# Attention layer in fp32 on one core: orders at both ends of the slot loop, and the tail's row work dealt out anew

## The reference

```python
Q = split_heads(query @ Wq + bq)
K = split_heads(key @ Wk + bk)
V = split_heads(value @ Wv + bv)
attn = softmax(einsum('bhqd,bhkd->bhqk', Q, K) / np.sqrt(D_K))
ctx = einsum('bhqk,bhkd->bhqd', attn, V).transpose(0, 2, 1, 3).reshape(B, S, D_MODEL)
out = ctx @ Wo + bo
return _layer_norm(out + query, ln_gamma, ln_beta)
```

## Time and profile before

| | us |
|---|---|
| median of 3 runs | 647.02 (645.25 to 647.41) |
| profiled execution | 653.13, its span 651.3 |
| last matmul ends | 632.3 |
| last GpSimd instruction ends | 648.05 |
| chain that ended last, over the span | GpSimd 37%, TensorE 31%, issue 18% |
| one slot in the middle | about 8.25 |

### The profile page before, as it was taken

One profiled execution on the slowest core, in us unless ns is written; L12 is line 12 of the kernel. 1 busy time (PEld: TensorE's weight loads), 2 busy tenths in 40 slices (PEclk: granted clock), 3 DMA queues, 4 the chain that ended last, 5 costly groups with the idle time before them and its releaser, 6 DMA issues.

```text
span 651.3 us, 12015 instructions
## 1 busy us (share of the span) xinstructions
PE 602.2 (92%) x3336; PEld 438.8 (67%) x3336; DVE 498.8 (77%) x909; ACT 361.7 (56%) x667; POOL 452.8 (70%) x401
## 2 busy tenths in 40 slices
PE   6989878999899999999999999999999999998980
PEld 5978645677676776777777777767777677675660
DVE  5523467888688888888888888888888888687655
ACT  5611145466466666666666666666666666554531
POOL 1433134448687887887888888888888878566697
PEclk9999978999899999999999999999999999898895
DMA  8758686978969898979798989797989899677212
GB/s 323 286 206 204 171 222 145 194 181 190 206 173 214 205 224 206 217 200 220 186 232 201 221 202 225 197 231 192 226 211 224 213 208 212 168 175 192 96 61 100
DMA packets 93392, 129.58 MB, mean 199 GB/s; under 512 B 49936, under 2 KB 49936, under 8 KB 93360
## 3 DMA queue, kind: packets, MB, share of 16 engines
q1 hardware_dynamic: 74352, 93.89, 59.1%
q10 hardware_dynamic: 19008, 35.30, 20.1%
HBM read 53.94 MB, written 24.35 MB: 120 GB/s over the span
## 4 chain that ended last, share of the span: by engine, by line
POOL 37%; PE 31%; issue 18%; DVE 3%; SPq 2%; ACT 1%; ACTq 1%; POOLq 1%; DMA 1%; DVEq 0%
PE p_q L579 11%; PE p_o L643 9%; POOL y L1003 8%; POOL xn L1019 8%; POOL xl L993 7%; POOL y L1007 6%; PE p_s L609 4%; POOL cl L1012 4%; POOL rstd L999 3%; PE p_v L622 2%; PE p_a L595 2%; PE p_o L99 1%; PE p_v L99 1%; SPq L538 1%; ACTq L783 1%
## 5 line engine op out<-in xcount | busy, mean ns | idle before, releaser
L708 ACT ACTIVATE prob<-p_s 77x512 f32<-77x512 f32 x256 | 143.6, 592 | 116.6 <-PE p_s L609 108.8
L1012 POOL TENSOR_TENSOR cl<-cxt,ch 128x512 fp32r<-128x512 f32 x64 | 83.2, 1300 | 125.9 <-ACT ch L733 125.9
L897 DVE TENSOR_REDUCE nm<-p_a 128x4 f32<-128x308 f32 x256 | 116.2, 475 | 60.5 <-PE p_a L595 59.0
L839 DVE TRANSPOSE_TENSOR_REDUCE part<-prob 96x64 f32<-96x2048 f32 x64 | 146.4, 2287 | 9.4 <-ACT prob L708 8.1
L723 ACT ACTIVATE qh<-p_q,bq_col 128x512 fp32r<-128x512 f32 x64 | 44.0, 687 | 126.2 <-PE p_q L579 126.2
L609 PE MATMUL p_s<-z,ks 97*77 97x512 f32 x256 | 97.3, 421 | 16.3 <-ACT prob L708 7.2
L579 PE MATMUL p_q<-xh,wqh 128*128 128x512 f32 x256 | 102.0, 398 | 1.7 <-PEq L151 1.7
L579 PE MATMUL p_q<-xl,wqh 128*128 128x512 f32 x256 | 102.2, 399 | 0.0
L579 PE MATMUL p_q<-xh,wql 128*128 128x512 f32 x256 | 101.7, 397 | 0.0
L993 POOL TENSOR_TENSOR xl<-xt,xh 128x512 fp32r<-128x512 f32 x60 | 77.4, 1290 | 29.4 <-ACT xh L715 29.4
L643 PE MATMUL p_o<-woh,ch 128*128 128x512 f32 x240 | 96.9, 404 | 0.1
(11 more groups left out here) (122 smaller groups left out, 937.2 us busy)
## 6 DMA issues: line engine op xcount, KB each, us to landing
z<-qh SPq DMA_DIRECT2D x240, 128.0 KB, 4.5
z<-ql SPq DMA_DIRECT2D x128, 128.0 KB, 4.4
xn<-in_x ACTq DMA_DIRECT2D x60, 256.0 KB, 3.7
out_dram<-y SPq DMA_DIRECT2D x60, 256.0 KB, 2.7
xt<-in_x_t ACTq DMA_DIRECT2D x58, 256.0 KB, 4.6
ks<-k_high SPq DMA_DIRECT2D x32, 154.0 KB, 3.7
cx<-in_ctx_t SPq DMA_DIRECT2D x4, 616.0 KB, 5.4
k_high<-kth SPq DMA_DIRECT2D x4, 616.0 KB, 3.5
```

Of the source, the lines that this page charges most:

```text
L708: nc.scalar.activation(prob[0:S2, j, :], p_s[j % 2][0:S2, :], ACT.Exp, scale=SCALE).then_inc(prob_ready, 1)
L839: nc.vector.tensor_reduce(part[:], prob[0:KP, :, :].rearrange("p h (i r) -> p (h i) r", r=DK), AX_X, ALU.add, apply_transpose=True).then_i ...
L897: nc.vector.tensor_reduce(nm[:, t, g.k % 2:HALF:2], p_a[t % 2][:, 0:HC * S2].rearrange("p (h k) -> p h k", k=S2), AX_X, ALU.max, negate=Tr ...
L1012: nc.gpsimd.tensor_tensor(cl[:, i, g.k % NCH, :], cx[:, g.k % 2, :], ch[:, i, g.k % NCH, :].bitcast(F32), ALU.subtract).then_inc(cl_ready, 1)
```

## The change

At the start, ScalarE issues its 8 copies of z in slot 3 behind the four `exp`, not ahead of them. At the end (slots 58 to 67 and behind):

- the four `x_last` loads go from SyncE (slot 63) to ScalarE's queue (slots 58, 59, 60 and 63), and GpSimd's four `add_bo_last` from slots 65 to 68 to slots 60, 61, 62 and 64;
- in slots 64 to 66 TensorE does two `scores` first, then `values`, then two `project_out`, and only then the softmax sums; VectorE does `add_residual` ahead of `sum_keys`;
- the last slot of ScalarE, VectorE and GpSimd is written out. ScalarE copies gamma and beta into two PSUM banks that are free by then. VectorE finishes tiles 58, 59, 62 and 63 with these copies; 60 and 61 go by ScalarE and GpSimd, and VectorE adds beta to 61. GpSimd's full-width steps behind the last `ctx_low` are four: `shift` of 57, `scale` and `shift` of 60, `scale` of 61;
- `bn_stats` and `bn_aggr` go: the addition itself sums its rows and ScalarE squares (`square_last`).

```diff
 # TensorE, slot(g)
-                if v.valid(NG):
+                if v.valid(NG) and g.valid(NG):
                     values(v)
+                    sums(v)
                 if s.valid(NG):
                     scores(s, 0)
                     scores(s, 1)
+                if not g.valid(NG):
+                    values(v)
                 for kc in range(KC):
+                    if kc == 2 and not g.valid(NG):
+                        sums(v)
                     if o.valid(NS):
                         project_out(o, kc)
-                    if s.valid(NG) and kc in (1, 2):
+                    if s.valid(NG) and g.valid(NG) and kc in (1, 2):
                         scores(s, kc + 1)
+                    if s.valid(NG) and not g.valid(NG) and kc in (2, 3):
+                        scores(s, kc)
 # ScalarE, slot(g)
-                if g.k % 2 == 1 and by_act(g.back(1)):
-                    ...    # 8 x act.dma_start(z, qh)
                 if s.valid(NG):
                     exp(s, 0)
                     exp(s, 1)
...
                     exp(s, 3)
+                if g.k % 2 == 1 and by_act(g.back(1)):
+                    ...    # the same 8
...
+                t = last_tile(g.back(LAG_LOAD_X))
+                if t is not None and t < QT - 1:
+                    load_last(t)
+                if last_tile(g.back(-1)) == 0:
+                    load_last(QT - 1)
 # ScalarE, behind slot 66
-            normalize(Slot(0, NS - 2))
+            act.wait_ge(prob_ready, NG * HC)
+            nc.scalar.copy(gamma_tail[:], gamma[:]).then_inc(rows_tail, 1)
+            square(Slot(0, NS - 2))
+            normalize(Slot(0, NS - 3))
+            act.wait_ge(rec_ready, NG)
+            nc.scalar.copy(beta_tail[:], beta[:]).then_inc(rows_tail, 1)
+            ctx_high(Slot(0, NG - 1))
             square(Slot(0, NS - 1))
-            for m in range(NS - 1, NS + ON_POOL):
-                normalize(Slot(0, m))
+            square_last(0)
+            square_last(1)
+            square_last(2)
+            normalize_last(0)
+            square_last(3)
+            normalize_last(1)
 # VectorE
+            def add_last(t):
...
+                nc.vector.scalar_tensor_tensor(out=x_last[t], in0=last_banks[t][0][:], scalar=0.0, in1=x_last[t],
+                                               op0=ALU.add, op1=ALU.add, accum_out=ysum[:, t, :]).then_inc(y_ready, 1)
+            def center_scale(m, n):
+                minus_mean(m, n)
...
+                nc.vector.scalar_tensor_tensor(out=rows(Slot(0, m)), in0=rows(Slot(0, m)), scalar=nmean[:, m % 4, :],
+                                               in1=gamma_tail[:], op0=ALU.add, op1=ALU.mult).then_inc(y_last_scaled, 1)
...
+            add_residual(Slot(0, NS - 2))
+            sum_keys(Slot(0, NG - 1))
+            minus_mean_over_std(Slot(0, NS - 3))
+            invert_sums(Slot(0, NG - 1))
+            divide(Slot(0, NG - 1))
+            variance_of_squares(Slot(0, NS - 2))
+            add_residual(Slot(0, NS - 1))
+            center_scale(NS - 2, 0)
+            variance_of_squares(Slot(0, NS - 1))
+            center_scale(NS - 1, 1)
+            divide_shift(NS - 2, 0)
             add_last(0)
+            divide_shift(NS - 1, 1)
             add_last(1)
+            variance_of_squares(Slot(0, NS))
             add_last(2)
+            variance_of_squares(Slot(0, NS + 1))
+            minus_mean_over_std(Slot(0, NS))
             add_last(3)
+            variance_of_squares(Slot(0, NS + 2))
+            minus_mean_over_std(Slot(0, NS + 1))
+            center_scale(NS + 2, 2)
+            variance_of_squares(Slot(0, NS + 3))
+            center_scale(NS + 3, 3)
+            divide_shift(NS + 2, 2)
+            divide_shift(NS + 3, 3)
+            shift_last(1)
 # GpSimd
-                t = last_batch_chunk(g, LAG_PV + 1)
-                if t is not None:
+                t = last_tile(g.back(LAG_SPLIT + 1))
+                if t is not None and t < QT - 1:
                     add_bo_last(t)
+            add_bo(Slot(0, NS - 1))
+            scale(Slot(0, NS - 4))
+            shift(Slot(0, NS - 4))
+            scale(Slot(0, NS - 3))
+            inverse_std(Slot(0, NS - 2))
+            ctx_low(Slot(0, NG - 1))
+            inverse_std(Slot(0, NS - 1))
+            shift(Slot(0, NS - 3))
+            inverse_std_last(0)
+            inverse_std_last(1)
+            scale_last(0)
+            inverse_std_last(2)
+            pool.wait_ge(scaled, NS - 1)
+            nc.gpsimd.tensor_tensor(x_last[0], x_last[0], beta[:], ALU.add).then_inc(y_done, 1)
+            inverse_std_last(3)
+            scale_last(1)
```

More of the change, by code:

```diff
@@ L447, in attend, with run @@
         p_vp = [p_o, p_v]
-        def run(engine, slot):
+        def run(engine, slot, end=NG + LAG_PV):
             loop_from, loop_to = 2, NG // PAIR - 1
@@ L457, in run @@
                     slot(Slot(u, k))
-            for k in range(PAIR * loop_to, NG + LAG_PV):
+            for k in range(PAIR * loop_to, end):
                 slot(Slot(k // PAIR, k % PAIR))
@@ L555, in _ @@
             run(sp, slot)
[L557 to L563, removed]
+            store(Slot(0, NS - 3))
+            for m in (NS - 2, NS - 1):
+                sp.wait_ge(y_last_done, m - NS + 3)
+                sp.dma_start(out_dram[m], y[:, m % 4, :]).then_inc(stored[m % 4], 16)
+            sp.wait_ge(y_done, NS - 1)
+            sp.dma_start(out_dram[NS], x_last[0]).then_inc(stored[0], 16)
+            for n, t in enumerate((2, 3, 1)):
+                sp.wait_ge(y_last_done, n + 3)
                 sp.dma_start(out_dram[NS + t], x_last[t]).then_inc(stored[t], 16)
@@ L794, in slot @@
                     exp(s, 3)
+                if g.k % 2 == 1 and by_act(g.back(1)):
+                    i = g.k // 2 % 2
+                    act.wait_ge(qh_ready, g.over(1, 1))
+                    for part in range(2):
+                        for j in range(HC):
+                            act.dma_start(z[DK * part:DK * (part + 1), i, j, :, :].bitcast(F32),
+                                          qh[DK * j:DK * (j + 1), i, :, :].bitcast(F32)).then_inc(z_in[i], 16)
                 if v.valid(NG):
@@ L917, in slot @@
                 v, m = g.back(LAG_PV), g.back(LAG_NORM)
+                if m.valid(NS) and not g.valid(NG):
+                    add_residual(m)
                 if v.valid(NG):
@@ L946, in add_last @@
                 dve.wait_ge(xb_last_ready, t + 1)
[L947 to L953, removed]
-                nc.vector.scalar_tensor_tensor(out=x_last[t], in0=x_last[t], scalar=mv[:, t, 0:1], in1=gamma[:],
-                                               op0=ALU.subtract, op1=ALU.mult).then_inc(y_last_scaled, 1)
@@ L958, in divide_shift @@
-            def divide_shift(t):
-                dve.wait_ge(rstd_ready, NS + t + 1)
-                dve.wait_ge(y_last_scaled, t - ON_POOL + 1)
-                nc.vector.scalar_tensor_tensor(out=x_last[t], in0=x_last[t], scalar=rstd[:, t, :], in1=beta[:],
-                                               op0=ALU.mult, op1=ALU.add).then_inc(y_last_done, 1)
-            m = Slot(0, NS - 1)
-            minus_mean_over_std(Slot(0, NS - 2))
-            add_residual(m)
-            variance_of_squares(m)
+                dve.wait_ge(squared, NS - 4 + t + 1)
@@ L976, in _ @@
             add_last(3)
-            divide_shift(2)
-            center_scale(3)
-            divide_shift(3)
+            variance_of_squares(Slot(0, NS + 2))
[6 more added lines that the diff above has]
+            shift_last(1)
         @block.gpsimd
@@ L1046, in slot, with scale_last, inverse_std_last @@
                                             keep["woh"][:, kc, :].bitcast(F32), ALU.subtract).then_inc(wo_low, 1)
-            run(pool, slot)
-            add_bo_last(QT - 1)
-            last = {t: Slot(0, NS + t) for t in range(-3, QT)}
-            scale(last[-3])
-            shift(last[-3])
-            inverse_std(last[-1])
-            scale(last[-2])
-            shift(last[-2])
-            inverse_std(last[0])
-            scale(last[-1])
-            inverse_std(last[1])
-            shift(last[-1])
-            inverse_std(last[2])
-            scale(last[0])
-            inverse_std(last[3])
-            shift(last[0])
-            scale(last[1])
-            shift(last[1])
+            run(pool, slot, NG + LAG_PV - 1)
+            def scale_last(t):
+                pool.wait_ge(normed, NS - 2 + t + 1)
+                nc.gpsimd.tensor_tensor(x_last[t], x_last[t], gamma[:], ALU.mult).then_inc(scaled, 1)
+            def inverse_std_last(t):
+                if t < 2:
+                    pool.wait_ge(normed, NS - 4 + t + 1)
+                else:
+                    pool.wait_ge(y_last_done, t - 1)
+                inverse_std(Slot(0, NS + t))
+            add_bo(Slot(0, NS - 1))
[14 more added lines that the diff above has]
+            scale_last(1)
 def xattn(nc, a, out):
```

83 lines of the change are left out of this document (47 added, 36 removed).

## The result

The changed kernel is faster, but by less than half of what was forecast: 643.64 us median of 20 runs (638.07 to 647.56) against 647.89 of 20 runs of the kernel before, ratio 0.994 with a 95% interval of 0.9914 to 0.9966, so 3.9 us (2.2 to 5.6). The forecast was 636.5, 10.5 us less than before. The profiled execution took 647.12, its span is 645.3.

A forecast was written before the change was run, and what follows sets the result against it. GpSimd was taken to set the end, and ScalarE's copies ahead of `exp` to hold TensorE at the start. Gains 2.4 + 8.1 = 10.5 us off the 647.02 median gave 636.5; own range 634.4 to 638.9, whole range 633.5 to 640.5.

The forecast's parts named there:

- The start: Slots 3 and 4: TensorE let go 6.1 us earlier, but `q_high(4)` waits behind the same issues; gain 2.4 us.
- The low clock of slot 5: Start: TensorE's new wait may bring a low clock into slot 5's products, cutting the gain to 1.5 us.
- Loads and additions: Slots 58 to 68: moved loads and GpSimd additions let the last maxima be issued 1.7 us earlier.
- TensorE's order: Slots 64 to 67: the rearranged slots by themselves bring nothing; TensorE ends at 631.8 against 632.3.
- one stretch of low clock: Slots 65 to 67, after the idle stretch: slower matmuls cost 1.5 us; ends none and 2.9 us.
- S: End of the last `ctx_low` (chunk 63): forecast 629.0, ends 627.5 and 630.5, against 627.94 before.
- S moved by over 1.5 us: Tail: one of the signs named as showing the prediction wrong, a shift of the last `ctx_low`'s end.
- Behind S: After the last `ctx_low`: GpSimd sets the pace, last step 11.4 us later, then 2.8 us to the span's end.
- Rival 1: Tail: passes still hold GpSimd up or VectorE is held up, with S at 630.5; gain 7.0, 640.0; chance 0.14.
- Rival 2: Start brings nothing, for instance if issues are slower beside SyncE's ks loads; gain 8.1, 638.9; chance 0.12.
- Rival 3: Slots 65 to 67 and behind: the clock stays low through the tail, slower, 652; chance 0.03.

The follow-up runs named there:

- front_only: Kernel before with one edit: ScalarE's 8 copies of z in slot 3 put behind the four `exp`; ratio 0.9982 to the kernel before.
- old_loads: Changed kernel with the old slot orders, and the `x_last` loads and GpSimd's `add_bo_last` back in their old places; ratio 0.9856 to the kernel before.
- split: Changed kernel with four of ScalarE's eight copies of z in slot 3 given to SyncE; ratio 0.9883 to the kernel before.
- fill: Changed kernel with 20 matmuls whose result nothing reads put ahead of `scores(62)` in slot 65; ratio 0.9896 to the kernel before.
- old_order: Changed kernel with the old slot order of TensorE and VectorE in slots 64 to 67; ratio 0.9818 to the kernel before.
- late: Changed kernel with TensorE's slot 65 reordered: `project_out`, `values` and sums ahead of `scores(62)`; ratio 0.9829 to the kernel before.
- sbuf: Changed kernel with VectorE's finishing passes reading gamma and beta from SBUF, ScalarE's PSUM copies kept unread; ratio 0.9954 to the kernel before.

## Why the prediction was wrong

- **The start: the second term that was mis-sized.** The mechanism held: TensorE let go 6 us earlier, and most of it lost again to `q_high(4)` behind the same issues. The term was 2.4 us; from `q_high(3)` to `q_high(8)` it measured 1.4 in the changed kernel's profile and 0.4 in front_only's, and from the span's start 0.5 on average. The eight issues took 6.85 us (0.54 + 6.31) in place of 5.68, which the prediction took over from before, and `q_high(4)` came 1.1 us later than forecast (11.36 against 10.3 behind `q_high(3)`). The low clock of slot 5, named as the other end (1.5), came: in the changed kernel it took no more than the low clock of slot 6, which went, and in front_only 0.9 more.
- **Loads and additions.** The direction held: `z<-nmt` was issued about 1.8 us earlier relative to `q_high(63)` (11.18 us after it against 13.02), 1.7 forecast, and `scores(62)` began 16.8 us after it, 18.2 before. The close match is in part luck: in the second profile of the kernel before, and in front_only's, the issue comes at 12.35 and 12.24, and `scores(62)` began at 17.8 to 18.5 with the loads where they were, at 16.8 to 18.0 in the four kernels with the moved loads that wait for z in slot 65 with the scores first. old_loads puts the part at 2.6 us, which one profile of each does not show.
- **TensorE's order: the step that failed.** The prediction saw the idle stretch ahead of `scores(62)`, wrote "an idle stretch of 4 to 5 us" (5.20 measured), and put in one stretch of low clock at 1.5 us, S 1.1 us later than before. S came 4.5 us later (5.3 in split's profile), and with that the sign that it named, S moved by over 1.5 us, came true. The low stretch was 7.8 us, longer than its wide end of 6.3, and it hit `values` too (1.94 in place of 1.06), which the count of matmuls had at 0.9. By fill it cost 3.1 to 3.5 us, where the sum had 1.5 and its wide end 2.9. The term put the clock wrong and not the wait: `scores(62)` began 16.8 us after `q_high(63)`, 16.5 by the forecast. Behind it lay a mis-weighted choice: the new order was taken as harmless because the work behind the wait fitted. The orders of old_order and late show that the wait need not be there: 38.8 and 37.65 us.
- **Behind S.** Held, and better than forecast: 13.34 us against 14.2, from 23.36. `add_last` in one pass, four GpSimd steps left behind S, VectorE not the bound. No disturbance with PSUM operands; sbuf shows the 2.0 us that it would have been, and 1.0 more ahead of S, where the prediction did not look for it.
- **The account.** Between the two first profiles, 0.2 us up to `q_high(8)`, 0.3 in the middle, 4.5 lost up to S and 10.0 won behind it make the 6.0 us by which the spans differ (651.3 and 645.3). The timed runs show 3.9.
- **The rivals.** Rival 1's held-up passes did not come, its late S did and went past its end. Rival 2, that the start brings nothing, came near: its own reason, slower issues, is what was measured, and front_only's ratio has 1 in its interval. Rival 3 was right about where the clock would fall and wrong only in how long: it was priced as all or nothing. A case between, one longer low stretch at 3 to 4 us, was missing, and the range ended at 640.5 for want of it.

Open: how much of the timed 3.9 us is start and how much tail, and why it is less than the profiles' 6.0, since the middle's own spread is 9 us in the profiles; why the eight issues took longer behind the `exp`; and why TensorE's granted clock came back after 7.8 us here and after 3.5 elsewhere.

## What to carry to other kernels

In an in-order engine, an instruction that may wait for a transfer belongs behind all work that is ready, and an order that fits the middle of a loop has to be looked at anew where transfers come late. Price a new idle stretch of TensorE twice, once as time and once as the slower matmuls behind it. A store that is moved later holds its buffer longer: look who writes that buffer next.

## What the runs showed of the hardware

- After TensorE had stood still 5.20 us, its granted clock was 0.50 for 7.8 us; with 20 unread matmuls of 4.82 us in that place it stayed at 1.00, and S came 3.1 to 3.5 us sooner after the start of `scores(62)`. The ratio was 0.9896 against 0.994, with intervals that overlap.
- A VectorE pass over two SBUF operands beside a GpSimd step took 1.74 us in place of 0.75, and the GpSimd step behind it 0.99 in place of 0.55; with one operand in PSUM it took 0.75, undisturbed. The Trainium skill (SBUF — State Buffer, section Who interferes with whom) states this lock, and these rows agree. PSUM made the pass itself no faster: 0.75 in both.
- Eight issues of ScalarE's queue took 5.68 us ahead of the `exp` of slot 3, with SyncE issuing copies for 2.6 us of it, and 6.85 behind them, where SyncE issues its own copies for all of that time. That the one causes the other is not shown.
